# Reordering the prologue of a slot-attention block: low parts of two weight chunks, a constant of the first layer, and one of three encoder groups

## The reference

```python
# first layer: attention on a window of the context, Luong style
score = einsum('nqh,hk,nlk->nql', layernorm(x), W_a, ctx)      # masked outside p +- 16
align = softmax(score) * exp(-(l - p) ** 2 / 128)
x = x + tanh(concat([align @ ctx, layernorm(x)]) @ W_c.T)
# second layer: 64 slots
S = slot_init
h = gelu(concat([layernorm(x), mean(S)]) @ w1 + b1)            # mean(S) is one row
logits = (h @ w2 + b2) / (abs(tau) + 0.1)
alpha = softmax over the 8 largest of the logits
# slot sums, a GRU cell on them (Wih, Whh), attention among slots, layernorm, then
out = (alpha @ (y @ wvp + bvp)) @ wo + bo
x = x + out
```

## Time and profile before

| what | us |
|---|---|
| median of 3 executions | 348.28 |
| lowest, highest | 347.82, 348.68 |
| span of the profiled execution, first to last instruction | 345.3 |
| TensorE busy in that span | 328.8 (95%) |
| VectorE, ScalarE, GpSimd busy | 249.3, 200.6, 209.5 |

### The profile page before, as it was taken

How to read it: one execution, slowest core, us unless ns; L and a number is a source line. 1 busy time by engine, 2 the same in 40 slices (tenths; PEclk the granted TensorE clock), 3 DMA queues, 4 the chain that set the end, 5 groups by cost and what they waited for, 6 DMA issues and landing times.

```text
span 345.3 us, 7118 instructions
## 1 busy us (share of the span) xinstructions
PE 328.8 (95%) x2320; PEld 284.0 (82%) x2320; DVE 249.3 (72%) x749; ACT 200.6 (58%) x406; POOL 209.5 (61%) x353
## 2 busy tenths in 40 slices
PE   8999998999999999999999999989999999999980
PEld 6697856999898989989989989977889886777750
DVE  5589897666787777878877877766944765578872
ACT  3567226477759679578587777676853345323420
POOL 5600247879687876875885785737674336136772
PEclk9999999999999999999999999999999999999996
DMA  7999866242424242232232300009700000000898
GB/s 274 277 348 388 296 194 208 68 122 63 121 64 122 62 125 64 72 113 61 84 101 63 91 5 2 0 0 338 251 2 1 0 2 0 0 2 1 323 345 307
DMA packets 40934, 42.79 MB, mean 124 GB/s; under 512 B 3245, under 2 KB 32045, under 8 KB 40898
## 3 DMA queue, kind: packets, MB, share of 16 engines
q1 hardware_dynamic: 38944, 40.19, 35.2%
q10 hardware_dynamic: 1666, 1.49, 1.3%
q0 software_dynamic: 288, 0.66, 0.6%
HBM read 32.18 MB, written 8.39 MB: 117 GB/s over the span
## 4 chain that ended last, share of the span: by engine, by line
PE 57%; POOL 11%; DVE 9%; issue 8%; ACT 6%; DMA 6%; SPq 1%; POOLq 0%; ACTq 0%; DVEq 0%
PE psum L456 13%; PE psum L457 13%; PE psum L458 13%; PE psum L1741 4%; PE psum L2003 3%; POOL hT_lo L599 3%; DMA xT<-in_xT 3%; PE psum L1770 3%; DMA encw<-in_enc,rowi 2%; PE psum L1721 2%; POOL X L604 2%; ACT th L1320 2%; POOL r2all L610 1%; PE psum L1805 1%; PE psum L1952 1%
## 5 line engine op out<-in xcount | busy, mean ns | idle before, releaser
L456 PE MATMUL psum<-GW_hi,hT_hi 128*128 128x292 f32 (+1 forms) x256 | 78.5, 307 | 0.0
L458 PE MATMUL psum<-GW_lo,hT_hi 128*128 128x292 f32 (+1 forms) x256 | 73.9, 289 | 0.0
L457 PE MATMUL psum<-GW_hi,hT_lo 128*128 128x292 f32 (+1 forms) x256 | 73.9, 289 | 0.0
L604 POOL TENSOR_TENSOR X<-X,th 128x512 f32<-128x512 f32 x32 | 38.2, 1193 | 28.4 <-ACT th L1320 28.4
L456 PEld LDWEIGHTS psum<-GW_hi,hT_hi 128*128 128x128 f32 x256 | 48.4, 189 | 1.4 <-issue 1.2
L457 PEld LDWEIGHTS psum<-GW_hi,hT_lo 128*128 128x128 f32 x256 | 48.3, 189 | 0.0
L458 PEld LDWEIGHTS psum<-GW_lo,hT_hi 128*128 128x128 f32 x256 | 48.1, 188 | 0.0
L971 DVE BATCH_NORM_STATS2 st<-X 128x6 f32<-128x512 f32 x32 | 22.2, 693 | 26.7 <-POOL X L604 26.6
L599 POOL TENSOR_TENSOR hT_lo<-xT,hT_hi 128x512 fp32r<-128x512 f32 x30 | 39.1, 1304 | 2.0 <-DVE stack L982 2.0
L456 PE MATMUL psum<-xhT_hi,w_hi 128*128 128x256 f32 x128 | 37.9, 296 | 0.8 <-issue 0.5
L457 PE MATMUL psum<-xhT_hi,w_lo 128*128 128x256 f32 x128 | 36.1, 282 | 0.0
(11 more groups left out here) (316 smaller groups left out, 909.6 us busy)
## 6 DMA issues: line engine op xcount, KB each, us to landing
xT<-in_xT SPq DMA_DIRECT2D x32, 256.0 KB, 2.9
X<-in_x SPq DMA_DIRECT2D x32, 256.0 KB, 3.5
out<-ost SPq DMA_DIRECT2D x32, 256.0 KB, 3.0
WhhT<-in_WhhT SPq DMA_DIRECT2D x1, 3072.0 KB, 12.7
WihT<-in_WihT SPq DMA_DIRECT2D x4, 768.0 KB, 8.6
Wo<-in_wo ACTq DMA_DIRECT2D x4, 256.0 KB, 3.0
WvpT<-in_WvpT SPq DMA_DIRECT2D x4, 256.0 KB, 3.7
WaT<-in_WaT SPq DMA_DIRECT2D x1, 1024.0 KB, 11.1
```

The costliest lines, as they stand in the source:

```text
L456: pe.matmul(out, w_hi, m_hi, start=start, stop=False)
L457: pe.matmul(out, w_lo, m_hi, start=False, stop=False)
L458: return pe.matmul(out, w_hi, m_lo, start=False, stop=stop)
L604: pool.tensor_tensor(tile_x(r), tile_x(r), halves(th[:, :]), ALU.add).then_inc(S("x2"), 1)
```

## The change

Three things move, and some with them.

1. The low parts of the two split chunks of `wvp` and `wo` are subtracted on VectorE, ahead of the last steps of its masks, and no longer on GpSimd. The row sums `wsum` move behind the masks and the load of the flag.
2. The constant of the first layer leaves the prologue of TensorE. In step 1, behind `bias_row`, four products of 32 rows and 256 columns (`smz` by `w1b`, one for each chunk, into four row groups of `H1`) replace the 8 products of one column. ScalarE copies them out (`hrow`), two products with a column of ones sum the groups in step 2, and VectorE adds `b1` in step 3. The load of `w1b` moves behind the first four tiles; its place takes the first half of `Wc2_raw`.
3. Of the encoder groups two stand ahead of the loop (`EARLY_VALUES`), and the third is computed in step 0 behind tile 0's products, with its high part on ScalarE behind `high_x(2)` and its low part on VectorE behind `stats1(2)`.

With them: the product of `wcs` stands ahead of the last chunk of `G`; the centered weights are made ahead of `G_lo`; ScalarE makes `encWT_hi` behind the first of the four `WaT_hi`; the two parts of `w1` are split between ScalarE (high, step 1) and VectorE (low, step 2); and the one wait for all of `split` becomes a wait for each chunk in tile 0's scores.

```diff
-        sp.dma_start(w1b[:, :, :], chunks("w1", KC)).then_inc(S("in_w1b"), 16)
+        sp.dma_start(Wc2_raw[:, 0:2, :], chunks("WcT", KC, 2)).then_inc(S("in_wc2"), 16)
         sp.wait_ge(S("encw"), 16 * NG)
-        sp.dma_start(Wc2_raw[:, :, :], chunks("WcT", KC)).then_inc(S("in_wc2"), 16)
+        sp.dma_start(Wc2_raw[:, 2:KC, :], chunks("WcT", KC + 2, 2)).then_inc(S("in_wc2"), 16)
         sp.dma_start(Wc1T[:, :, :], chunks("WcT")).then_inc(S("in_wc1"), 16)
         for t in range(4):
             xT_load(t)
             x_load(t)
+        sp.dma_start(w1b[:, :, :], chunks("w1", KC)).then_inc(S("in_w1b"), 16)
...
-        for n, k in enumerate(SPLIT_WP):
-            pool.wait_ge(S("wa"), 2 * n + 1)
-            pool.tensor_tensor(Wvp_lo[:, n, :], WvpT[:, k, :], Wvp_hi[:, n, :].bitcast(F32), ALU.subtract).then_inc(S("wcs"), 1)
-            pool.wait_ge(S("wa"), 2 * n + 2)
-            pool.tensor_tensor(Wo_lo[:, n, :], Wo[:, k, :], Wo_hi[:, n, :].bitcast(F32), ALU.subtract).then_inc(S("wcs"), 1)
...
-        v.wait_ge(S("in_wa"), 16)
-        for c in range(2, KC):
-            v.tensor_reduce(wsum[:, c:c + 1], WaT[:, c, :], AX.X, ALU.add).then_inc(S("v_prep"), 1)
+        for n, k in enumerate(SPLIT_WP):
+            v.wait_ge(S("wa"), 2 * n + 1)
+            v.tensor_tensor(Wvp_lo[:, n, :], WvpT[:, k, :], Wvp_hi[:, n, :].bitcast(F32), ALU.subtract).then_inc(S("v_prep"), 1)
+            v.wait_ge(S("wa"), 2 * n + 2)
+            v.tensor_tensor(Wo_lo[:, n, :], Wo[:, k, :], Wo_hi[:, n, :].bitcast(F32), ALU.subtract).then_inc(S("v_prep"), 1)
...
-        v.wait_ge(S("pre"), HB_DONE)
-        v.tensor_tensor(hb[:, :], banks[3][:, 0:HC], b1, ALU.add).then_inc(S("first_row"), 1)
...
+        v.wait_ge(S("pre"), WM_DONE)
+        for k in range(KC):
+            v.tensor_tensor(Wc2_raw[:, k, :], Wc2_raw[:, k, :], banks[7], ALU.add).then_inc(S("split"), 1)
         for c in range(KC):
             v.wait_ge(S("pre"), G_DONE + c + 1)
...
-            if s == 1:
-                v.wait_ge(S("in_w1"), 16)
-                link(v.tensor_copy(w1_hi[:, :, :], w1_raw[:, :, :]), "w1s")
-                link(v.tensor_tensor(w1_lo[:, :, :], w1_raw[:, :, :], w1_hi[:, :, :].bitcast(F32), ALU.subtract), "w1s")
+            if s == 2:
+                v.wait_ge(S("w1s"), 1)
+                v.tensor_tensor(w1_lo[:, :, :], w1_raw[:, :, :], w1_hi[:, :, :].bitcast(F32), ALU.subtract).then_inc(S("w1s"), 1)
+            if s == BIAS_STEP + 2:
+                v.wait_ge(S("pre"), HB_DONE)
+                v.tensor_tensor(hb[:, :], H1[:, HALF:HALF + HC], b1, ALU.add).then_inc(S("first_row"), 1)
...
+            if s == 0:
+                for g in range(EARLY_VALUES, NG):
+                    high_values(g)
+            if s == BIAS_STEP:
+                act.wait_ge(S("pre"), HB_PARTS)
+                act.copy(hrow[:, :], H1[:, 0:DH]).then_inc(S("wa"), 1)
+                act.wait_ge(S("in_w1"), 16)
+                act.copy(w1_hi[:, :, :], w1_raw[:, :, :]).then_inc(S("w1s"), 1)
...
-        pe.wait_ge(S("in_w1b"), 16)
-        pe.wait_ge(S("v_prep"), MEAN_DONE)
-        for o in range(HC):
-            for k in range(KC):
-                last = pe.matmul(banks[3][:, o:o + 1], w1b[:, k, o * P:(o + 1) * P], slotmean[:, k:k + 1],
-                                 start=k == 0, stop=k == KC - 1)
-        last.then_inc(S("pre"), 1)
...
         for k in range(KC):
+            if k == KC - 1:
+                pe.wait_ge(S("v_prep"), CHUNKS_DONE)
+                pe.wait_ge(S("wp"), KC)
+                pe.matmul(banks[7], cmean[:, :], wcs[:, :], start=True, stop=True).then_inc(S("pre"), 1)
             pe.wait_ge(S("encWT"), LOW_WA[k])
...
+            if s == 0:
+                for g in range(EARLY_VALUES, NG):
+                    encoder_values(g)
...
+                pe.wait_ge(S("wa"), HI_HB)
+                for o in range(HC):
+                    last = pe.matmul(H1[:, HALF + o:HALF + o + 1], hrow[:, o * P:(o + 1) * P], ones[:, 0:1], start=True, stop=True)
+                last.then_inc(S("pre"), 1)
...
+            pe.wait_ge(S("v_prep"), SLOT_MEAN_DONE)
+            pe.wait_ge(S("in_w1b"), 16)
+            pe.wait_ge(S("ew"), 2)
+            for k in range(KC):
+                last = pe.matmul(H1[32 * k:32 * (k + 1), 0:DH], smz[:, k, :], w1b[:, k, :], start=True, stop=True)
+            last.then_inc(S("pre"), 1)
...
+                if s == 0:
+                    pe.wait_ge(S("split"), KC + c + 1)
...
-        pe.wait_ge(S("split"), 2 * KC)
```

More of the change, by code:

```diff
@@ L324, in program @@
     flagf, vlo = early("flagf", 1), early("vlo", NB * WS)
+    smz = place("smz", [P, KC, 32], F32, "early2")
+    hrow = place("hrow", [P, DH], F32, "early2")
     assert cursor["early2"] <= at_of("w1")
@@ L791, in _ @@
         v.tensor_scalar(gw[0:WP, :], gw[0:WP, :], geo[:, 1:2], None, ALU.max).then_inc(S("first_row"), 1)
-        v.wait_ge(S("in_misc"), 16 * 4)
-        link(v.tensor_reduce(slotmean[:, :], slotT[:, :, :], AX.X, ALU.add), "rt")
-        v.tensor_scalar(slotmean[:, :], slotmean[:, :], 1.0 / NS, None, ALU.mult).then_inc(S("v_prep"), 1)
         v.wait_ge(S("flag"), 1)
         f = v.value_load(flag[0:1, 0:1], min_val=0, max_val=NB)
+        v.wait_ge(S("in_wa"), 16)
+        for c in range(2, KC):
+            v.tensor_reduce(wsum[:, c:c + 1], WaT[:, c, :], AX.X, ALU.add).then_inc(S("v_prep"), 1)
         def windows(j):
@@ L851, in _ @@
             v.tensor_tensor(G_lo[:, c, :], src, G_hi[:, c, :].bitcast(F32), ALU.subtract).then_inc(S("g_lo"), 1)
-        v.wait_ge(S("pre"), WM_DONE)
-        for k in range(KC):
-            v.tensor_tensor(Wc2_raw[:, k, :], Wc2_raw[:, k, :], banks[7], ALU.add).then_inc(S("split"), 1)
         low_x(0)
@@ L1032, in step @@
                 scores_max(s)
-                if s == 0:
-                    low_values(2)
                 if live(s + 3) and s:
@@ L1043, in step @@
             if s == 0:
+                low_values(2)
                 stats1(3)
@@ L1260, in _, with high_key_weights @@
         link(act.mul(wneg[:, :], wsum[:, :], -1.0 / D))
-        for c in range(KC):
+        def high_key_weights(c):
             act.activation(WaT_hi[:, c, :], WaT[:, c, :], ACT.Identity, bias=wneg[:, c:c + 1]).then_inc(S("wa"), 1)
+        high_key_weights(0)
         for j in range(1, ENC_BANKS):
@@ L1265, in _ @@
             act.copy(bank_windows(encWT_hi, j), banks[j][:, 0:ENC_COLS]).then_inc(S("wa"), 1)
+        for c in range(1, KC):
+            high_key_weights(c)
         for c in range(KC):
@@ L1567, in _ @@
                 n = SPLIT_WP.index(k)
-                pe.wait_ge(S("wcs"), 2 * n + 2)
+                pe.wait_ge(S("v_prep"), 2 * n + 2)
             for c in range(KC):
@@ L1620, in _, with encoder_values @@
                     last.then_inc(S("pre"), 1)
-        pe.wait_ge(S("v_prep"), CHUNKS_DONE)
-        pe.wait_ge(S("wp"), KC)
-        pe.matmul(banks[7], cmean[:, :], wcs[:, :], start=True, stop=True).then_inc(S("pre"), 1)
-        for g in range(NG):
+        def encoder_values(g):
             at_g = slice(g * WP, (g + 1) * WP)
@@ L1632, in _ @@
             last.then_inc(S("pre"), 1)
+        for g in range(EARLY_VALUES):
+            encoder_values(g)
         def extras(s):
+            if s == 0:
+                for g in range(EARLY_VALUES, NG):
+                    encoder_values(g)
             if s == GATES_STEP:
@@ L1761, in turn_rows @@
             pe.wait_ge(S("xn"), r + 1)
+            if r == 0:
+                pe.wait_ge(S("ew"), NG)
             if r == NT - 1:
```

38 lines of the change are left out of this document (23 added, 15 removed).

## The result

| | before | changed |
|---|---|---|
| median | 348.05 us (4 executions) | 344.65 us (4 executions) |
| lowest, highest | 347.25, 348.68 | 344.14, 346.24 |
| span of the profiled execution | 345.3 us | 342.7 us |

The ratio is 0.9912, 95% interval 0.9891 to 0.9934: 3.1 us faster (2.3 to 3.8). (The two medians differ by 3.4 us, which lies within that interval.) The forecast was 345.9 us, between 345.0 and 347.5.

What follows compares the result with a forecast made beforehand. TensorE, busy 95% of the span, sets the time: -1.70 + 0.50 + 0.43 - 0.53 - 0.20 - 0.9 = -2.4 us, so span 342.9 plus 3.0 around it gives 345.9 us; range 345.0 to 347.5.

Steps and rivals of the forecast that it cites:

- That is the real gain: VectorE's prologue: masks and flag load fit in before 14.3 us, so first windows are rounded 2.5 us sooner.
- The tie of VectorE (39.4) and TensorE (39.6): Tile 0's turned weights: VectorE ready at 39.4 us, TensorE there at 39.6, so the 0.53 us gap closes.
- The flag on TensorE: Flag's load and branch, now behind matmuls of 0.23 us each: priced 0, from above 0.76 us.
- -1.70: TensorE's prologue: the one-column product goes, 1.70 us less.
- -0.53: TensorE at tile 0's turned weights: its gap of 0.53 us closes.
- Worth nothing on TensorE: Split chunks' low parts moved to VectorE: first pair at 10.8 us, not near 11.4, but no wait stood there.
- Steps 0 to 3: Passage on TensorE's loop: new products +0.50 and sums over `hrow` +0.43 us; waits of 0.20 and 0.99 mostly go.
- the wait of 0.20: TensorE at the first transposes of normalized rows: rows ready near 50.3 us, arrival 52.8, so the 0.20 us goes.
- the wait of 0.99: TensorE at tile 1's normalized rows: rows and arrival both at 57.0 us, so 0.9 of the 0.99 counted as gone.
- step 3: Fourth step of the loop: the prediction's sum has no term for a change in its length.
- more comes through: Rival: a later TensorE gap of 0.5 to 1.0 us closes too; 345.2 us, chance 0.08.
- The slower rival: TensorE stops 1.5 us before the column means, its clock falls, 2.5 us of work take 5; 349.9 us, chance 0.04.

Runs made afterwards that it cites:

- Run 4: Changed kernel with the row sums over `WaT` back ahead of the masks, the flag and its load; 346.40 us, ratio 0.9958 to the kernel before.
- run 2: Changed kernel with `EARLY_VALUES` = 3, all three encoder groups ahead of the loop; 343.94 us, ratio 0.9896 to the kernel before.
- Run 7: Changed kernel with the earlier load order and slot mean, one-column products and `hb` back in the prologue, without step 1's products and step 2's sums; 345.96 us.
- run 11: Changed kernel with three products of the last split chunk ahead of the encoder transposes; 344.37 us, ratio 0.9908 to the kernel before.
- run 3: Changed kernel with the four low parts of the split chunks back on GpSimd; 345.90 us, ratio 0.9937 to the kernel before.
- run 10: Changed kernel with the four low parts of the split chunks back on GpSimd, measured again; 346.04 us, ratio 0.9951 to the kernel before.
- run 12: Changed kernel with six products of the last split chunk ahead of the encoder transposes; 344.78 us, ratio 0.9919 to the kernel before.
- run 5: Changed kernel with the earlier load order: `w1b` ahead of the gather, both halves of `Wc2_raw` behind it; 345.59 us, ratio 0.9946 to the kernel before.

## Why the prediction was right and where it was wrong

**The place of the gain: right.** Of the masks and the flag, which now fit in ahead of `WaT`'s landing, the prediction said "That is the real gain": VectorE's first windows come 2.48 us sooner (3.08 to 0.60), forecast 2.5. Run 4 undoes it alone and loses 2 us. Tile 0's turned weights, counted from the transposes, come at 24.30 instead of 26.59: 2.29 us sooner, where the steps gave 2.28 (39.6 for 41.88). The tie of VectorE (39.4) and TensorE (39.6) there was also right, by `stack`'s end at 40.46 and the turn at 40.51. The flag on TensorE, priced 0 against 0.76, cost 0. That group 2 is moved and not saved held (run 2). But the sum books these 2.3 us as TensorE's (-1.70 and -0.53). Runs 7 and 11 show that VectorE's chain carries them: putting the 1.70 us back costs at most 0.4 us, and taking another 0.68 us away gains nothing. That both ways of counting gave the same time was the tie, and in part luck. `Wc1T` came 1.05 us sooner where 1.4 was forecast, and the slack behind it was used up: VectorE waited 0.16 us for it.

**"Worth nothing on TensorE": the low parts were priced too low.** The row of 1.49 us got no price, as VectorE stood idle behind it. The move's real worth is that VectorE's masks finish in time at all: without it the new order loses 1.6 to 1.7 us (runs 3, 10).

**The step that failed: the passage "Steps 0 to 3" of the prediction.** From tile 0's to tile 4's turned weights the sum was +0.50 + 0.43 - 0.20 - 0.9 = -0.17 us. Measured: 25.09 - 25.87 = -0.78. By its terms, from start to start:

| term | forecast | measured |
|---|---|---|
| new products behind `bias_row` | +0.50 | +0.44 (0.54 for them, `bias_row` itself 0.11 less) |
| sums over `hrow` | +0.43 | +0.43 |
| the wait of 0.20 | -0.20 | -0.59 |
| the wait of 0.99 | -0.9 | -0.80 |
| step 3 | 0 | -0.26 |

The rows of the kernel before that this is counted from:

```profile
52.11 1.95 PE L1648 MATMUL psum<-WhhT,slotT 128*64 128x256 f32 x16
...
54.92 0.37 PE L456 MATMUL psum<-GW_hi,hT_hi 128*128 128x292 f32 x1
...
58.13 0.40 PE L1805 MATMUL psum<-EW,aTs 108*128 108x256 f32 x2
...
60.14 0.37 PE L456 MATMUL psum<-GW_hi,hT_hi 128*128 128x292 f32 x1
...
67.75 0.27 PE L1795 MATMUL psum<-ident,stack 128*108 128x128 f32 x1
```

The mechanism was right and the size of the stops was off, and step 3 was put at nothing. I took a stop as its bracket. But from the `WhhT` products to the scores behind tile 0's normalized rows it was 2.81 us before and 2.29 now: the stop of 0.20 cost 0.52. A restart's first instructions are longer (transposes to scores 0.66 instead of 0.41), and 0.08 us more lay ahead of the `WhhT` products. The stop of 0.99 was larger, too, but only a part of it closed. From the `aTs` products ahead of it to the scores behind tile 1's rows it was 2.01 us before and is 1.22 now. The like stretch without any stop takes 0.66 (0.25 from 50.84 to 51.09 and 0.41 from 53.40 to 53.81). So the stop cost 1.35 us, and 0.56 of it remains; the brackets of the weight loads (0.24 and 0.34) show it. In step 3 three handovers (`aTs` to the first product of `xhT_hi`, from there to the transposes of `ghs`, and from the transposes of `xh` to the scores) took 0.33, 1.50 and 0.45 us and now take 0.24, 1.43 and 0.35, with no bracket in either kernel. Run 7 has 0.37, 1.50 and 0.45 again, so this term belongs to the constant's new place, which the prediction priced only as added work. Runs 4, 10 and 12 say the same of longer stops: from transposes to scores they need 1.77, 1.80 and 2.40 us more than the 16.64 of the changed kernel (15.26 for run 12, whose 1.38 us stand ahead of the transposes), with brackets of 1.06, 1.08 and 1.67. That is about 0.36 us a stop above its bracket, as at the stop of 0.99 (1.35). So the rival "more comes through" came nearest (345.2 us), though the gap that it meant was in no row.

**The second miss: the base.** 345.3 plus 3.0 is the median 348.28 again, so the forecast is that median less 2.4 us, and it stands on three executions. In 54 more of the kernel before the medians of the three sets were 347.67, 347.54 and 347.17, so the base was 0.6 to 1.1 us high. The 3.0 us are not a time around the span either. The profile belongs to none of these three executions: only the fourth of the result, 347.25 us, is above the span of 345.3 by as much (1.95) as the other executions of this kernel are above theirs (1.85 to 2.08). By the ratio the change is -3.1 us, and from transposes to tile 4 it is -3.07, so about 0.6 of the 1.25 us between forecast and time is the base and the rest the steps.

**The range was too narrow below.** It began 0.9 us below the forecast. The steps were 0.6 us short, which it would have held; with the base's error on top the time fell outside it. Single executions of the changed kernel had spans between 341.9 and 344.4.

**The slower rival** didn't come as forecast; but run 3's profile shows its mechanism at another place: two stops ahead of the transposes, then 3 us at half clock, and 1.6 us lost instead of the 2.5 forecast for the slow stretch. It decides nothing here: in the three profiles of the changed kernel the stop is one, of 0.6 to 1.2 us, and the clock stayed at 1.00 from there to the scores.

**Settled and open.** The masks' order is 2.0 to 2.2 us of the 3.1, and keeping the low parts off GpSimd protects 1.6 to 1.7 of the same. Against the order of before, the load order is 0.9 to 1.4 us (run 5), as cover for what part 1 uncovers. The constant's new place is between nothing and 0.4 us, group 2's is none. These are losses on undoing one part, so they don't add up. Run 7 ties step 3's shorter handovers to the constant's new place; by which path it shortens them is open. So is how much of the loss of runs 3 and 10 comes from each of their two mechanisms.

## What to carry to other kernels

Look for the one supplier whose distance to the next milestone is constant over all variants: here tile 0 came 23.5 us behind VectorE's first windows in nearly every kernel, so only what moved those windows paid, and TensorE's own work ahead of tile 0 was nearly free. Put work that needs nothing ahead of a transfer's landing. Count a stop start to start between the same two instructions, not by its idle bracket. A forecast in us stands on the base as much as on the steps: a median of three executions can be off by more than the effect of a step.
